# Writing out the first two passes and the last one of a software-pipelined attention kernel

## The reference

```
L0: q = x Wq; k, v = enc Wk, enc Wv          (enc: the first 124 context tokens; 8 heads)
    hs  = softmax(q k' / sqrt(d)) v
    ca  = the last 4 context tokens; ca_q1 = (ca' Wq_ca) at 128 of 192 channels
    c1  = attention(ca_q1, x, x)
    hs2 = attention(c1 Wq, ca Wk_ca, ca Wv_ca)
    x   = (hs + hs2) Wout + b + x
L1: x = attention(LN1 x, LN1 x) o1 + x       (20 heads of 16)
    x = attention(LN2 x, context) o2 + x     (20 heads of 16)
    a, g = split(LN3 x ff_w1 + b1)
    x = (a * gelu(g)) ff_w2 + b2 + x
```

## Time and profile before

| | |
|---|---|
| median of three runs | 3696.13 us |
| profiled execution | 3700.3 us, span 3698.4 us |
| TensorE matmul busy | 93% of the span |
| DVE, ACT, POOL busy | 61%, 67%, 56% |
| mean granted TensorE clock | 0.956 of full |
| a pass of the loop | about 108 us |

### The profile page before, as it was taken

One profiled execution on the slowest core, in us unless ns is written; L12 is line 12 of the kernel. 1 busy time (PEld: TensorE's weight loads), 2 busy tenths in 40 slices (PEclk: granted clock), 3 DMA queues, 4 the chain that ended last, 5 costly groups with the idle time before them and its releaser, 6 DMA issues.

```text
span 3698.4 us, 114778 instructions
## 1 busy us (share of the span) xinstructions
PE 3427.4 (93%) x38842; PEld 2788.6 (75%) x38842; DVE 2269.9 (61%) x5540; ACT 2494.6 (67%) x4428; POOL 2070.6 (56%) x2307
## 2 busy tenths in 40 slices
PE   7899999999999999999999999999999999999999
PEld 7677787777777777777777777787777777777777
DVE  6566666566566656666655666665566666556665
ACT  3576676767767676776767677676767767676774
POOL 1565555556655555655555566555556655555664
PEclk6899999999999999999999999999999999999999
DMA  5211111221111122111112211111221111112111
GB/s 185 56 42 44 40 43 48 50 53 46 47 44 42 45 50 52 46 47 42 43 46 50 52 46 47 42 43 46 50 52 46 47 42 43 45 50 52 46 47 26
DMA packets 316267, 183.06 MB, mean 49 GB/s; under 512 B 50107, under 2 KB 315379, under 8 KB 315507
## 3 DMA queue, kind: packets, MB, share of 16 engines
q1 hardware_dynamic: 303936, 173.93, 18.5%
q10 hardware_dynamic: 11955, 3.04, 0.4%
HBM read 70.59 MB, written 24.67 MB: 26 GB/s over the span
## 4 chain that ended last, share of the span: by engine, by line
PE 44%; issue 20%; POOL 11%; DVE 7%; SPq 6%; ACT 5%; DMA 5%; POOLq 1%; ACTq 1%; DVEq 0%
PE bank L1487 41%; SPq L406 5%; DMA Qs<-cQ 5%; DVE mx L1104 4%; PE bank L1514 2%; ACT PT L811 2%; POOL rstd L598 2%; POOL cK L547 1%; POOL cQ L547 1%; ACT L794 1%; POOL c L592 1%; ACT P L810 1%; POOL X L517 1%; POOL rstd L597 1%; PE bank L1609 1%
## 5 line engine op out<-in xcount | busy, mean ns | idle before, releaser
L540 POOL TENSOR_TENSOR PT<-P,PT 128x512 f16<-128x512 f32 (+1 forms) x924 | 1066.9, 1156 | 808.5 <-ACT PT L811 806.2
L1487 PE MATMUL bank<-hT,w_ff_w 128*128 128x256 f16 x5440 | 644.0, 273 | 29.3 <-DVE G L1018 29.3
L1104 DVE TENSOR_REDUCE mx<-bank 128x4 f32<-128x512 f32 (+1 forms) x924 | 588.5, 682 | 115.7 <-PE bank L1487 108.3
L1487 PEld LDWEIGHTS bank<-hT,w_ff_w 128*128 128x128 f16 x5440 | 518.3, 98 | 100.5 <-DVE G L1018 41.0
L1487 PE MATMUL bank<-mxs,pick 84*128 84x128 f16 (+1 forms) x3696 | 513.6, 223 | 0.0
L1183 DVE SCALAR_TENSOR_TENSOR F<-bank,ff_b,gate 128x256 f32<-128x256 f32 x340 | 160.0, 481 | 435.9 <-ACT gate L794 435.9
L1487 PE MATMUL bank<-w_ff,F 128*128 128x320 f32 x1360 | 418.4, 443 | 1.3 <-DVE F L1183 1.3
L1487 PEld LDWEIGHTS bank<-mxs,pick 84*128 84x128 f16 (+1 forms) x3696 | 380.6, 105 | 4.0
L1487 PE MATMUL bank<-Ks,Qs 96*128 96x128 f16 x2640 | 236.0, 235 | 148.3 <-DMA Qs<-cQ 144.3
L1487 PEld LDWEIGHTS bank<-V,PT 128*128 128x128 f16 (+1 forms) x9504 | 336.2, 96 | 48.7 <-issue 23.5
L1487 PE MATMUL bank<-Qs,Ks 96*128 96x128 f16 x2640 | 359.3, 219 | 11.2 <-DVE mxs L1113 7.3
(11 more groups left out here) (290 smaller groups left out, 7310.6 us busy)
## 6 DMA issues: line engine op xcount, KB each, us to landing
Qs<-cQ SPq DMA_DIRECT2D x402, 64.0 KB, 2.6
Ks<-scratch_k SPq DMA_DIRECT2D x99, 160.0 KB, 4.6
Ks<-cK SPq DMA_DIRECT2D x198, 64.0 KB, 2.6
Q0s<-cQ SPq DMA_DIRECT2D x198, 60.0 KB
K0s<-cK SPq DMA_DIRECT2D x198, 60.0 KB
xin<-in_x SPq DMA_DIRECT2D x34, 320.0 KB, 3.5
out<-X SPq DMA_DIRECT2D x64, 160.0 KB, 1.8
xT<-in_xT SPq DMA_DIRECT2D x68, 128.0 KB, 2.1
```

The costliest lines, as they stand in the source:

```text
L540: nc.gpsimd.tensor_tensor(PT[0:keys, n % PT_SLOTS, 1, :], P[0:keys, n % P_SLOTS, :], PT[0:keys, n % PT_SLOTS, 0, :], ALU.subtract).then_in ...
L1104: nc.vector.tensor_reduce(mx[:, g % 2, 4 * u:4 * u + 4], bank[:, :].rearrange("p (h s) -> p h s", h=4)[:, :, 0:keys], axis=AX.X, op=ALU.ma ...
L1487: return nc.tensor.matmul(o, lhsT, rhs, start=start, stop=stop)
```

## The change

Passes 0, 1 and 32 are written out as straight code on TensorE, DVE, ACT and POOL, without the calls that have no step there; the loop runs passes 2 to 31. What a left-out call would have added to the counters is added by `left_out`: on DVE, ACT and POOL a drain with the count, on TensorE a one-element matmul that waits for its bank to be free. In pass 0 there are 36 drains on DVE, 18 on ACT, 12 on POOL and 40 such matmuls on TensorE; in pass 1 9, 7, 0 and 11; in pass 32 41, 24, 13 and 34. SP keeps its copies in passes 0 and 1, and in pass 32 leaves out the load of token products and the ten loads of the next step. Since the integers 0, 1 and 32 are now pass numbers in Python, the tests `isinstance(i, int)` that marked the code ahead of the loop become `i < 0`.

```diff
-            def one_pass(i, stores):
+            def one_pass(i, stores, last=False):
...
-                load_products(i)
-                load_next(i)
+                if not last:
+                    load_products(i)
+                    load_next(i)
...
-            with sp.Fori(2, STEPS + 1) as i:
+            with sp.Fori(2, STEPS) as i:
                 one_pass(i, True)
+            one_pass(STEPS, True, True)
+            for landed in stacked["K0T"]:
+                sp.wait_ge(landed, (STEPS + 1) * 48)
...
+            def left_out(i, v_done_by=0, dve_done_by=0, o_done_by=0, var_ready_by=0, xh_ready_by=0, ext_ready_by=0, diag_ready_by=0, p4_ready_by=0):
+
+                if v_done_by:
+                    dve.drain().then_inc(v_done, v_done_by)
+                order.next += v_done_by
...
-            with nc.Fori(0, STEPS + 1, engines=[pe.engine], hint_back_edge=True) as i:
+            def left_out(i, j_full_by=0, pv_done_by=0):
+
+                n = min(filled[0], PER["J"] - 1)
+                bank_free(i, LOOP_JOBS, n)
+                o = j_bank[n % J_BANKS][0:1, 0:1]
+                if pv_done_by:
+                    mm(o, one_row[:, 0:1], one_row[:, 0:1]).then_inc(pv_done, pv_done_by)
+                if j_full_by:
+                    mm(o, one_row[:, 0:1], one_row[:, 0:1]).then_inc(j_full, j_full_by)
+                filled[0] += j_full_by
+
+            i = 0
+            L = LOOP_JOBS
+            filled[0] = 0
+            left_out(i, j_full_by=1)
+            chunk(i, "Q0T", 0, "Wq", x16, PASSES_X, AT0, CH0)
+            chunk(i, "Q0T", 1, "Wq", x16, PASSES_X, AT0, CH0)
+            left_out(i, j_full_by=1)
+            chunk(i, "Q0T", 2, "Wq", x16, PASSES_X, AT0, CH0)
+            left_out(i, j_full_by=4)
+            scores(i, 0)
+            scores(i, 1)
...
+            left_out(i, pv_done_by=1, j_full_by=1)
+            extremes_turned(i, L)
+            left_out(i, pv_done_by=2, j_full_by=5)
+            extremes_everywhere(i, L, 2)
+            left_out(i, pv_done_by=6, j_full_by=6)
+            chunk(i, "K0T", 1, "Wk", c16, PASSES_C, AT0, CH0)
+            left_out(i, j_full_by=3)
+            scores4(i)
+            left_out(i, j_full_by=6)
+            chunk(i, "K0T", 2, "Wk", c16, PASSES_C, AT0, CH0)
...
```

More of the change, by code:

```diff
@@ L638, in _ @@
+            token_queries(i)
+            assert links[0] == POOL_LINKS
+            with nc.Fori(2, STEPS, engines=[pool.engine], hint_back_edge=True) as i:
                 links[0] = 0
@@ new lines, in _ @@
+            high_tokens(i, L)
+            turn_factors(i, done(i, PER["V"] - 1, "V"))
+            assert order.next == PER["A"]
+            assert links[0] == ACT_LINKS
+            i = 1
+            L = LOOP_JOBS
+            order.restart()
+            links[0] = 0
+            left_out(i, a_done_by=1)
+            high_chunk(i, "Q0T", 0, cQ, CH0[0], FQ0)
+            high_chunk(i, "Q0T", 1, cQ, CH0[1], FQ0)
+            high_blocks(i, "XT0_0", hTn, 0)
+            high_chunk(i, "Q0T", 2, cQ, CH0[2], FQ0)
@@ new lines, in _ @@
+            high_out(i, 2, 1)
+            exps(i, 26)
+            exps(i, 27)
+            high_out(i, 0, 0)
+            first_part(i, "V2", 1, V2, HEADS1, D1, fixed[:, F2:F2 + 1])
+            high_out(i, 0, 1)
+            high_blocks(i, "XT2_0", hT3, 0)
+            high_blocks(i, "XT2_1", hT3, 1)
+            high_tokens(i, L)
+            turn_factors(i, done(i, PER["V"] - 1, "V"))
+            assert order.next == PER["A"]
+            assert links[0] == ACT_LINKS
+            with nc.Fori(2, STEPS, engines=[act.engine], hint_back_edge=True) as i:
@@ L974, in _ @@
+            left_out(i, a_done_by=5)
+            high_blocks(i, "XT2_0", hT3, 0)
+            high_blocks(i, "XT2_1", hT3, 1)
+            left_out(i, a_done_by=1, act_done_by=1, factor_ready_by=1)
+            assert order.next == PER["A"]
+            assert links[0] == ACT_LINKS
             order.restart()
@@ new lines, in _ @@
+            i = 0
+            L = LOOP_JOBS
+            links[0] = 0
+            order.restart()
+            left_out(i, v_done_by=1)
+            low_chunk(i, "Q0T", 0, cQ, CH0[0], FQ0)
+            low_chunk(i, "Q0T", 1, cQ, CH0[1], FQ0)
+            left_out(i, v_done_by=1)
+            low_chunk(i, "Q0T", 2, cQ, CH0[2], FQ0)
+            left_out(i, v_done_by=4)
+            maxima(i, 0)
+            maxima(i, 1)
+            left_out(i, v_done_by=2)
+            maxima(i, 2)
+            maxima(i, 3)
@@ new lines, in _ @@
+            normalise(i, 7)
+            left_out(i, xh_ready_by=1)
+            whole_heads(i, 1)
+            left_out(i, xh_ready_by=1)
+            low_part(i, "V2", 1, V2, HEADS1, D1, fixed[:, F2:F2 + 1])
+            residual(i, 0, 0)
+            low_out(i, 0, 1)
+            left_out(i, v_done_by=2)
+            low_tokens(i, L)
+            residual(i, 0, 1)
+            norm(i, 0, 0)
+            norm(i, 0, 1)
+            assert order.next == PER["V"]
+            assert links[0] == STEP_LINKS, links[0]
@@ L1354, in _ @@
+            assert order.next == PER["V"]
+            assert links[0] == STEP_LINKS, links[0]
+            with nc.Fori(2, STEPS, engines=[dve.engine], hint_back_edge=True) as i:
                 L = LOOP_JOBS
@@ new lines, in _ @@
+            residual(i, 2, 0)
+            left_out(i, v_done_by=1)
+            residual(i, 2, 1)
+            left_out(i, v_done_by=1, dve_done_by=1, o_done_by=1)
+            norm(i, 2, 0)
+            left_out(i, v_done_by=1)
+            norm(i, 2, 1)
+            left_out(i, v_done_by=3, dve_done_by=1, var_ready_by=1)
+            low_blocks(i, "XT2_0", hT3, 0)
+            low_blocks(i, "XT2_1", hT3, 1)
+            left_out(i, v_done_by=2, dve_done_by=1, var_ready_by=1, xh_ready_by=2)
+            assert order.next == PER["V"]
@@ new lines, in _ @@
+            exponents(i, 1)
+            left_out(i, j_full_by=2)
+            scores(i, 4)
+            scores(i, 5)
+            exponents(i, 2)
+            token_values(i)
+            scores(i, 6)
+            scores(i, 7)
+            values1(i, 0)
+            exponents(i, 3)
+            attend(i, 0)
+            scores(i, 8)
+            attend(i, 1)
+            scores(i, 9)
+            turn_maxima(i, 2)
+            scores(i, 10)
+            chunk(i, "K0T", 0, "Wk", c16, PASSES_C, AT0, CH0)
@@ new lines, in _ @@
+            exponents(i, 4)
+            scores(i, 11)
+            attend(i, 2)
+            exponents(i, 5)
+            scores(i, 12)
+            scores(i, 13)
+            attend(i, 3)
+            exponents(i, 6)
+            values1(i, 1)
+            attend(i, 4)
+            turn_maxima(i, 3)
+            exponents(i, 7)
+            turn_ca(i, 0)
+            turn_ca(i, 1)
+            attend(i, 5)
+            exponents(i, 8)
+            extremes_turned(i, L)
+            attend(i, 6)
@@ new lines, in _ @@
+            scores(i, 14)
+            scores(i, 15)
+            left_out(i, j_full_by=1)
+            scores(i, 16)
+            scores(i, 17)
+            scores(i, 18)
+            values(i, "V0", 1, "Wv")
+            chunk(i, "K2T", 0, "k2", c16, PASSES_C, AT1, CH1)
+            turn_maxima(i, 4)
+            scores(i, 19)
+            scores(i, 20)
+            scores(i, 21)
+            exponents(i, 14)
+            scores(i, 22)
+            scores(i, 23)
+            chunk(i, "K2T", 1, "k2", c16, PASSES_C, AT1, CH1)
@@ new lines, in _ @@
+            scores(i, 27)
+            exponents(i, 22)
+            attend(i, 19)
+            attend(i, 20)
+            exponents(i, 23)
+            left_out(i, j_full_by=1)
+            attend(i, 21)
+            turn_maxima(i, 7)
+            exponents(i, 24)
+            exponents(i, 25)
+            attend(i, 22)
+            chunk(i, "K2T", 2, "k2", c16, PASSES_C, AT1, CH1)
+            attend(i, 23)
+            turn_out(i, 2, 0)
+            values(i, "V2", 0, "v2")
+            turn_out(i, 2, 1)
@@ L1799, in _ @@
+            out_proj(i, 0, 1)
+            assert filled[0] == PER["J"]
+            with nc.Fori(2, STEPS, engines=[pe.engine], hint_back_edge=True) as i:
                 L = LOOP_JOBS
```

959 lines of the change are left out of this document (952 added, 7 removed).

## The result

The changed kernel takes 3672.6 us, the median of four runs (3667.4 to 3676.5). Its ratio to the kernel before is 0.9936 [0.9921, 0.9952]: 18 to 29 us faster, about 24, where 44 were forecast. The profiled execution took 3667.4 us; against the one before that is 33 us.

A forecast was written before the change was run, and what follows sets the result against it. The bound was taken to be a long dependency chain across engines, SP included, rather than TensorE's busy time. Gains of 31 + 3.5 + 9 = 43.5 from 3700.3, less 4.2 for the runs, gave 3652 us; range 3636 to 3661, wider 3630 to 3674.

The forecast's parts named there:

- Pass 0, 31 forecast: Pass 0 without feed-forward and attentions 1 and 2 ends near 185 instead of 216.2, 31 us gained; bounds 20 and 38.
- The path through SP: Pass 0: SP's copies, still issued in the old order, followed one after another up to S25 and T24 at 167.5.
- the last term: End of pass 0: T24 to the last matmul, 16.24 us before, taken as 17.5 with part at lower clock.
- Pass 1, 3.5 forecast: Pass 1 without its feed-forward part: 6.2 less 4, plus 1 for gelu's table loads, 3.5 us gained.
- The gains ahead of S4 and behind T13: Pass 1: S4 comes 1.5 us earlier; behind T13, feed-forward work no longer delays outT1_1 and Q2T, 2.2 us.
- The two new holes take back 2 each at the lower clock: Pass 1: TensorE idles behind T13 and before S14, then runs slower; 4 us taken off the gain.
- The rival on the clock: Passes 1 and 32 at 1.2 GHz throughout, 37 and 26 us longer; kernel 38 slower, 3734; chance 0.03.
- Pass 32, 9 forecast: Pass 32 without first attention, token path and next step's loads: 11.5 less 2.5, 9 us gained; bounds 4 and 20.
- Less 2.5 for a cold start of the tail: End of pass 32: a new hole leaves the tail starting at lower clock, 2.5 us off the gain.
- The loop, 0 forecast: The 30 passes in the loop keep their code and time, staying at 108 us; nothing summed for them.
- The gain is small: Waits stay in pass 0 (20), pass 1 gives nothing, pass 32 gives 4; time 3672 to 3686; chance 0.12.
- a stall at the back edge: Loop's back edges: three fewer taken branches might save at most 2.3 us; by the trace nothing, none added.

The follow-up runs named there:

- no_p1: The changed kernel with pass 1 run in the loop again, passes 0 and 32 still written out; 3665.6 us, ratio 0.9917.
- p0_only: The changed kernel with only pass 0 written out, passes 1 to 32 in the loop; 3667.4 us, ratio 0.9924.
- warm1: The changed kernel with unread TensorE matmuls in pass 1, shaped like the left-out feed-forward ones, at their places; 3640.2 us, ratio 0.9851.
- fill_loop: fill_and_skip with unread matmuls where TensorE waits: 128 in pass 0, 88 in pass 32, 26 per loop pass ahead of S4; 3613.4 us, ratio 0.9790.
- fill_and_skip: The changed kernel with TensorE filled in pass 1 and SP's unread copies left out in passes 0 and 32; 3628.6 us, ratio 0.9827.
- pad_after: The changed kernel with 99 more waits near the start of TensorE's queue, which only move its later code; 3653.4 us, ratio 0.9877.
- drains: The changed kernel with five drains in place of each of 66 in pass 0 on DVE, ACT and POOL; 3673.5 us, ratio 0.9946.
- sp_skip: The changed kernel with SP also leaving out unread copies, 30 in pass 0 and 21 in pass 32; 3670.2 us, ratio 0.9935.
- tuned: fill_loop with its loop 18 places earlier, 22 unread matmuls ahead of S4, 6 ahead of mT, and changed filling in passes 0 and 1; 3583.4 us, ratio 0.9687.
- pad_before: The kernel before the change with 196 more waits on TensorE's queue, putting its loop where warm1 has it; 3684.7 us, ratio 0.9974.

## Why the prediction was half right

- **Pass 0, 31 forecast, 28.8 came** (33.4 in no_p1 and p0_only). The path through SP held step by step: free at 134 (133.6), next loads landed at 142.5 (142.3), K0T1 copies at 148.5 (148.95), S25 at 163 (162.92), T24 at 167.5 (168.1). Only the last term was short: T24 to the last matmul took 19.1 us, not 17.5, with the granted clock at 0.55 over the pass. The same code of pass 0 took 84.7 to 89.3 us in six kernels, so part of the near hit is luck.
- **Pass 1, 3.5 forecast, -2.5 came.** The gains ahead of S4 and behind T13 were there (2.4 and 3.5 us of lead). The step that failed is "The two new holes take back 2 each at the lower clock". The stretches behind several holes went at 0.5 to 0.8, the window of the pass had 0.83 for "near 0.9", and warm1 puts the whole effect at 6.1 us. The rival on the clock had the right sign for this pass; the loss was 6 us where it needed 37. S0 did not wait long for POOL's ca_heads as I had it: the row of that wait has 0.22 us.
- **Pass 32, 9 forecast, 1.8 came.** "Less 2.5 for a cold start of the tail" was mis-sized in the same way: the clock of the stretch fell from 0.98 to 0.89. The stall of 2.35 us at the loop's exit was not in the sum either, but the kernels that have pass 32 written out and no stall end no sooner. With the holes filled (fill_loop, which also leaves out SP's copies there) the stretch is 134.7 us, 6.7 less than in fill_and_skip and 7.4 less than before: near the 9.
- **The loop, 0 forecast.** It held (3229.8 for 3233.5), but by luck: "The 30 passes in the loop keep their code and their time" is wrong as a rule. The same code took 3199 to 3241 us according to the kernel around it. At the place of warm1 the change would have come out at 3643 (pad_after less its head), 53 us below the kernel before at its own place; 27 of these are the place's, for the kernel before would be at 3669 there too. The loop stood still here because both of its places, 102 and 199, put a packet among the Ks copies.
- **The rivals.** 3672.6 is also the near end of the rival that said "The gain is small" (3672 to 3686). It was right that pass 1 gives nothing and pass 32 little. It was wrong on pass 0, which gave 28.8 for its 20, and on the cost of left-out blocks. TensorE's busy time did not set the length: pass 1 lost 16 us of it and grew.
- **Instruction fetches.** I looked for a stall at the back edge and rightly found none. By the Trainium skill ("Runtime: NRT & Kernel Launch", "Instruction fetch mechanics"), code streams in 16 KiB blocks of 256 instructions, and crossing into a new one is mostly hidden. The trace agrees with the size (ten packets, 0.16 MB in a loop pass). On TensorE itself no stop shows: in the 30 loop passes of the kernel before, the changed one and warm1 every idle time over 0.3 us is ended by another engine or a DMA. But a packet that meets SP's row of nine issues makes that row 0.3 to 1.2 us longer (0.8 in the mean of the changed kernel). For a branch the Trainium skill ties the stall, in the same section, to a target outside a window of two blocks; no run here isolates that. At the exit the stall is there with the loop at 199 or 202 (2.3 to 2.6 us in six kernels) and absent at 102, 24, 42 and 43.
- **Left-out blocks, 0.5 forecast.** Not to be told from nothing, as drains shows for pass 0.

Open: why sp_skip's loop was 0.4 us a pass slower than the changed one's at the same place (its row of Ks copies takes 6.9 us in the mean for 6.55, and S4 comes 0.25 us later, so the packet costs more there), and why a packet holds up SP's issue. That the packets act through SP rests on the rows of both places; a fetch alone was not tried apart from the code's place.

## What to carry to other kernels

Before taking work out of an engine, ask whether it was what kept TensorE at full clock: here 28 idle matmuls a pass in two holes of the loop, with a place that suits them, took 38 us off the loop (fill_and_skip to tuned), and writing out three passes 24 off the kernel. After any edit that changes the number of instructions ahead of a loop, compare the loop's passes first, since the same code can run 1% faster or slower by where it lies; a trial with a few dozen idle instructions tells. A pass with one bound engine (SP in pass 0) was forecast to 2 us by adding up that engine's queue, and cutting the queue then gave 15 more; that second forecast was 6 us short.

## What the runs showed of the hardware

- Instruction packets of 16 KB for TensorE lengthen a row of nine of SP's copy issues from 5.8 us to 6.1 to 7.3 when they come among them (changed kernel and before, against pad_after and pad_before), and a pass of 108 us then takes 0.7 to 1.2 us more.
- Behind the loop's exit TensorE stood for 2.3 to 2.6 us nine matmuls later in the six kernels at places 199 and 202, and in none of the eight at other places. In the tail alone it made 4.2 us (p0_only); with pass 32 written out the time to the end was no shorter without it.
- Waits on counters long reached are not free: 99, 157 and 196 instructions of two waits each moved the first G by 10.4, 13.7 and 15.4 us, 0.08 to 0.1 us for an instruction.
- Five drains in a row where there was one cost nothing measurable in a pass with 66 such places, on engines that were busy for 25 to 35 of its 89 us.
- Matmuls that nobody reads shortened passes: pass 1 by 6.1 us with the granted clock from 0.83 to 1.00 (warm1), and the 30 loop passes by 38 us with the clock from 0.97 to 1.00 (fill_and_skip to tuned, the place moved too).
